# Last self attention in pairs of tiles, and expert results sent by stored numbers

## The reference, cut to what matters

```python
    def _L1_attn_ref(...):            # 16 heads of 128; w = codes * scales, blocks of 32 rows
        q = _mxfp4_matmul(x, wq_codes, wq_scales) + bq
        k = _mxfp4_matmul(x, wk_codes, wk_scales) + bk
        v = _mxfp4_matmul(x, wv_codes, wv_scales) + bv
        scores = jnp.einsum('bqhd,bkhd->bhqk', q, k) / jnp.sqrt(jnp.float32(HEAD_DIM))
        attn = jax.nn.softmax(scores, axis=-1)
        out = jnp.einsum('bhqk,bkhd->bqhd', attn, v).reshape(B, S, NUM_HEADS * HEAD_DIM)
        return _mxfp4_matmul(out, wo_codes, wo_scales) + bo

    def _L1_ffn_ref(...):             # 8 experts, each row goes to its 2 best
        probs = jax.nn.softmax(x @ gate_w, axis=-1)
        gate_score, gate_idx = jax.lax.top_k(probs, TOP_K)
        gate_score = gate_score / jnp.sum(gate_score, axis=-1, keepdims=True)
        combine = jnp.einsum('tk,tke->te', gate_score, onehot) * alpha[None, :]
        h = jax.nn.gelu(jnp.einsum('th,ehi->eti', x, fc1_w) + fc1_b[:, None, :], approximate=False)
        y = jnp.einsum('eti,eih->eth', h, fc2_w) + fc2_b[:, None, :]
        return jnp.einsum('eth,te->th', y, combine)
    ...
    x = x + _L1_attn_ref(_layernorm(x, axis=-1), ...)
    x = x + _L1_ffn_ref(_layernorm(x, axis=-1), ...)
```

## Time and profile before

| | |
|---|---|
| median of 3 runs | 2684.87 us (2684.1 to 2685.65) |
| the profiled execution, its own time | 2690.18 us |
| its span | 2688.5 us |
| mean granted clock of TensorE | 0.98 |
| PE busy | 2534.1 us, 94% |
| PEld busy | 1899.0 us, 71% |
| DVE busy | 1352.2 us, 50% |
| ACT busy | 1269.6 us, 47% |
| POOL busy | 740.1 us, 28% |

### The profile page before, as it was taken

One profiled execution on the slowest core, in us unless ns is written; L12 is line 12 of the kernel. 1 busy time (PEld: TensorE's weight loads), 2 busy tenths in 40 slices (PEclk: granted clock), 3 DMA queues, 4 the chain that ended last, 5 costly groups with the idle time before them and its releaser, 6 DMA issues. The chain is left out here.

```text
span 2688.5 us, 56576 instructions
## 1 busy us (share of the span) xinstructions
PE 2534.1 (94%) x16582; PEld 1899.0 (71%) x16582; DVE 1352.2 (50%) x4786; ACT 1269.6 (47%) x5189; POOL 740.1 (28%) x942
## 2 busy tenths in 40 slices
PE   6999999989899989998899999999879999999797
PEld 5888888878544444445577778777668888888675
DVE  3555555546577744445434455443424444444434
ACT  2555555544466766665546665546412222222142
POOL 1223232347355520003433333321050111111004
PEclk9999999999899999999999999999989999999898
DMA  5322222110510024422445543333280000000033
GB/s 182 78 62 62 65 66 66 53 45 0 166 48 2 1 71 133 128 57 60 131 111 125 138 110 100 96 87 91 99 204 5 8 8 8 8 8 8 18 97 114
DMA packets 171206, 196.01 MB, mean 73 GB/s; under 512 B 34028, under 2 KB 136617, under 8 KB 170307
## 3 DMA queue, kind: packets, MB, share of 16 engines
q1 hardware_dynamic: 142306, 158.49, 20.3%
q0 software_dynamic: 16512, 32.58, 5.4%
q10 hardware_dynamic: 12256, 3.44, 0.8%
HBM read 150.42 MB, written 56.54 MB: 77 GB/s over the span
## 5 line engine op out<-in xcount | busy, mean ns | idle before, releaser
L2276 PE MATMUL sa_work_ps<-sa_xnT,all_big 128*128 128x128 f32 x2048 | 239.7, 279 | 18.1 <-POOL all_big L2609 8.2
L228 PE MATMUL rt_kn_key_ps<-moe_w_wk,all_big 128*128 128x512 f32 x560 | 249.5, 599 | 0.8 <-DVE moe_kn_stats L277 0.4
L2276 PEld LDWEIGHTS sa_work_ps<-sa_xnT,all_big 128*128 128x128 f32 x2048 | 235.2, 195 | 20.5 <-POOL all_big L2609 8.7
L715 ACT ACTIVATE xa_probsT<-xa_probsT_ps 128x256 f32<-128x256 f32 x512 | 191.2, 375 | 95.4 <-PE xa_probsT_ps L580 89.1
L560 PE MATMUL xa_misc_ps<-xa_xnT,cross_folded 128*128 128x256 f32 x1024 | 232.7, 382 | 0.7 <-ACT xa_xnT L681 0.7
L603 PE MATMUL xa_misc_ps<-cross_folded,xa_mixT 128*128 128x256 f32 x1024 | 229.3, 379 | 0.0
L560 PEld LDWEIGHTS xa_misc_ps<-xa_xnT,cross_folded 128*128 128x128 f32 x1024 | 196.0, 191 | 31.5 <-ACT xa_misc_ps L690 3.3
L603 PEld LDWEIGHTS xa_misc_ps<-cross_folded,xa_mixT 128*128 128x128 f32 x1024 | 194.6, 190 | 26.5
L2369 ACT ACTIVATE sa_kT<-sa_work_ps,sa_bias_k 128x128 f32<-128x128 f32 x256 | 73.2, 368 | 294.7 <-PE sa_work_ps L2276 294.7
L580 PE MATMUL xa_probsT_ps<-all_ident,xa_probs 128*128 128x128 f32 x1024 | 197.6, 275 | 4.6 <-DVE xa_probs L841 3.7
L707 ACT ACTIVATE xa_probs<-xa_probs,xa_shift,xa_row_scale 128x257 f32<-128x257 f32 x256 | 152.6, 596 | 90.5 <-DVE xa_shift L825 89.7
(11 more groups left out here) (388 smaller groups left out, 4969.5 us busy)
## 6 DMA issues: line engine op xcount, KB each, us to landing
all_big<-rk SPq DMA_DIRECT2D x256, 128.5 KB
xa_pair<-pairs SPq DMA_DIRECT2D x64, 256.5 KB, 15.1
pairs<-all_big SPq DMA_DIRECT2D x64, 128.5 KB, 3.0
moe_w_wk<-in_ctx_dram SPq DMA_DIRECT2D x64, 128.0 KB, 2.5
pairs<-xa_keys SPq DMA_DIRECT2D x64, 128.0 KB, 2.2
cross_folded<-in_L_ffn_w_gate_dram SPq DMA_DIRECT2D x32, 192.0 KB, 2.5
cross_folded<-in_L_ffn_w_up_dram SPq DMA_DIRECT2D x32, 192.0 KB, 2.7
ff_rows<-pairs SPq DMA_DIRECT2D x35, 128.0 KB, 2.1
```

Source lines behind the costliest of these rows:

```text
L228: pe.matmul(self.key_ps[m % self.banks][0:n, :], self.ctxT[:, c * P:c * P + n], self.wk[:, q * 512:(q + 1) * 512], start=True, stop=True). ...
L715: act.activation(probsT[:, b % 2, :, r * P:(r + 1) * P], probsT_ps[s % 2][:, 0:KB * P].rearrange("p (k n) -> p k n", k=KB), ACT.Copy).then ...
L2276: ins = pe.matmul(ps[:, j, :], w[:, c, h * HD:(h + 1) * HD], xnT[:, c, :], start=(c == 0), stop=(c == NC - 1))
```

## The change

**Attention in pairs.** All working tiles of the attention hold two tiles of rows (`S` = 2, `NP` = 8 pairs). `project_qk` makes q and k for both at once, in eight groups of two heads with products 256 wide; `project_v`, `score`, `mix` and `project_out` run once for each tile of the pair. `iteration` makes q, k, v and scores of pair i + 1 and mix and output of pair i, once plainly and six times in the loop. Routing goes by pairs and one pair behind, so the last sparse pair (6) is routed after the loop, beside the last pair's mix and output. `count` has five small products a pair in place of two a tile. `list_tiles` now follows the last `keep_mix`.

**Sends by stored numbers.** `place` also makes for each choice a number that says where its result belongs (choice, tile, row). GpSimd scatters these numbers, beside the rows, into a second table `expert_ids`, which was filled with a number out of range before; that makes eight indirect DMAs a pair. In `last_experts` SyncE loads with each tile of rows its 128 numbers (two loads a tile, five tiles ahead), and GpSimd sends each `kept` buffer to `expert_out` by them (one indirect DMA a tile), in place of SyncE's store. When all are sent, SyncE loads `expert_out` back with 14 plain loads of 256 KB, two tiles and one choice each; the gathers are gone. `combine` stands behind `add` of experts 2 to 7, two tiles each, the last two after; output is stored two tiles at a time.

**Owners.** TensorE loads the owners' numbers of four tiles with one load, after `turn_rows` and ahead of `second`, in place of one load ahead of each `first`.

**Smaller parts.** The second weights of the feed-forward and the spread second bias are loaded into `spare` and `big`, when their former content is used up. ScalarE runs one Gelu on a gate column at the start of `last_experts`. `stats_of`, `normalize` and `weigh` of the two dense tiles are spread over more steps.

```diff
-ROWS_AHEAD = 6
+LIST = TILES + -TILES % 4
+NO_ONE = 65535
+ROWS_AHEAD = 5
...
-            def project_qk(n, first, route=False):
-                pe.wait_ge(xnT_ready, n + 1)
-                for g in range(NG):
...
+            def project_qk(p, first):
+                pe.wait_ge(xnT_ready, p + 1)
+                for m in range(NS):
+                    if first and m % 2 == 0:
+                        pe.wait_ge(scaled, m + 2)
+                    for w, ps, kept, made in ((wq, work(0, N), q_kept, q_made), (wk, work(1, N), k_kept, k_made)):
...
-            with pe.Fori(1, NT - 1) as i:
+            with pe.Fori(1, NP - 1) as i:
                 iteration(i, True)
-            pe.wait_ge(r_placed, RT)
-            pe.matmul(total_ps, ones[:, :], before[:, :], start=True, stop=True).then_inc(totalled, 1)
-            mix(NT - 1, True)
-            project_out(NT - 1)
+            turn_routed(NP - 2)
+            choose_experts(NP - 2)
+            mix(NP - 1, 0, True)
+            project_out(NP - 1, 0, NP - 2)
+            mix(NP - 1, 1, True)
+            total()
+            project_out(NP - 1, 1)
...
-                dve.wait_ge(scattered, n * (16 * TOP))
+                dve.wait_ge(scattered, p * (32 * TOP * S))
...
+                for t in range(S):
+                    for k in range(TOP):
+                        at = bass.IndirectOffsetOnAxis(ap=places[:, t, k:k + 1], axis=0)
+                        pool.indirect_dma_start(out=expert_rows, out_offset=at, in_=r_xn[:, t, :], in_offset=None,
+                                                bounds_check=E1 * ROOM - 1, oob_is_err=False).then_inc(scattered, 16)
+                        pool.indirect_dma_start(out=expert_ids, out_offset=at, in_=numbers[:, t, k:k + 1], in_offset=None,
+                                                bounds_check=E1 * ROOM - 1, oob_is_err=False).then_inc(scattered, 16)
...
+            def load_owners(j):
+                found = nc.values_load_multi_w_load_instructions(tiles[0:1, 0, j:j + 4], engines=(mybir.EngineType.PE,),
+                                                                 min_val=0, max_val=E1 - 1)[1]
...
             def first(j):
-                owners[j] = pe.value_load(tiles[0:1, 0, j:j + 1], min_val=0, max_val=E1 - 1)
...
+                if j % 4 == 3 and j + 1 < TILES:
+                    load_owners(j + 1)
...
+            act.activation(warmed[:, :], q["gates"][:, 0:1], ACT.Gelu)
...
-            for t in range(RT):
-                for k in range(TOP):
-                    pool.indirect_dma_start(out=got[:, t, k, :], out_offset=None, in_=expert_rows,
-                                            in_offset=bass.IndirectOffsetOnAxis(ap=q["slots"][:, t, k:k + 1], axis=0),
-                                            bounds_check=EXPERT_ROWS - 1, oob_is_err=False).then_inc(gathered[t], 16)
...
+            for j in range(TILES):
+                if j >= ROWS_AHEAD:
+                    pool.wait_ge(rows_loaded[j % ROWS_AHEAD], 32 * (j // ROWS_AHEAD))
+                pool.wait_ge(out_kept, j + 1)
+                apart(pool, passed)
+                pool.indirect_dma_start(out=expert_out, out_offset=bass.IndirectOffsetOnAxis(ap=ids[:, j:j + 1], axis=0),
+                                        in_=kept[:, j % KEPT, :], in_offset=None, bounds_check=TOP * ROOM - 1, oob_is_err=False
+                                        ).then_inc(kept_sent[j % KEPT], 16)
```

641 lines of the change are left out of this document (370 added, 271 removed).

## The result

| | before | after |
|---|---|---|
| median of the runs, us | 2685.26 (2684.1 to 2694.56, 4 runs) | 2716.6 (2715.46 to 2721.92, 4 runs) |
| ratio to before | 1 | 1.0111, 95% interval 1.0094 to 1.0128 |
| the profiled execution, its own time / span | 2690.18 / 2688.5 | 2717.19 / 2715.5 |
| mean granted clock of TensorE | 0.98 | 0.97 |

Left out are one of the two executions of the SyncE version in experiment 6 (3001 us, granted clock 0.84) and one of the kernel before beside it (3795 us, 0.65), both far slower than the same kernels otherwise run.

A forecast was written before the change was run, and what follows sets the result against it. TensorE was taken to bound the kernel, with GpSimd's gathers setting its end. Attention 1.2, sparse part 8.8 and end 11.4 sum to 21.4 us off 2690.2, less 5.3: 2663.5 us median, range 2654 to 2673.

The forecast's parts named there:

- Head: Start of the attention: projecting two tiles together ends the wait for scaled weights; plain iteration starts at 2007.1, gain 10.4 us.
- Loop: Attention loop: a pair takes 69.2 us, eight scatters hide under 69 us; with the head 18.2 us ahead.
- T: End of the last scores of the attention, predicted at 2489.4 us; the drain's steps are timed from it.
- Rival (d): Attention loop stalls: each of 16 groups a pair late by 0.2 us, 22 us, giving 2685.5 us; chance 0.06.
- Loop length: TensorE's attention loop grows from 191 to 321 instructions; by the skill's room for 2048, nothing changes.
- Drain: From the last scores to the next block: 54.3 us, a cost of 17.0 us, bounds 9 and 21.
- Sparse part: Sparse feed-forward, 35 tiles: owners loaded four at a time save 0.25 us a tile, 2.25 us each, gain 8.8.
- Rival (a): Sparse part as before: the load of four stops TensorE like four single ones, or mid waits otherwise; 2672.3 us; chance 0.12.
- (e): Slower: sends through GpSimd pace the sparse part, deciding from 8.2 us a send; 2706 us at 10; chance 0.05.
- End: End of the kernel: plain loads replace 28 gathers; 7.5 us behind TensorE instead of 18.9, gain 11.4.
- rival (c): Loads of results at the end are slow, 114 GB/s: 8.1 us late, 2671.6 us; chance 0.05.
- The sum: Whole kernel: gains of 1.2 + 8.8 + 11.4 = 21.4 us, giving 2668.8 us profiled, 2663.5 us median.

The follow-up runs named there:

- the SyncE version: Kernel before with two plain 128 KB stores more, issued by SyncE beside the scores of each of 14 tiles: 2679.0 us against 2685.4, a single execution.
- experiment 6: Plain stores beside scores: two by SyncE (2679.0 us) or GpSimd (2685.4) in the kernel before; fourteen by GpSimd in the changed kernel with scatters held back (2693.4).
- experiment 2: Kernel before with each tile's 64 score products issued twice: 2751.6 us; with TensorE's loop written out for two tiles: 2729.1 us against 2725.9, ratio 1.0004.
- experiment 1: Changed kernel with the pair's 128 scores split into two bursts of 64, v projection between: 2757.6 us, 1.0117 times before; the unaltered changed kernel took 2759.8.
- experiment 4: Changed kernel with both tiles' scores issued ahead of the count and the last output projection: 2711.4 us, 0.9944 times before, 48.4 less than the unaltered changed kernel.
- experiment 3: Changed kernel with GpSimd's scatters held back until the next pair's scores are through: 2720.7 us, 0.998 times before, 39 less than the unaltered changed kernel.
- experiment 7: Changed kernel with scores ahead of the count and the attention's end reordered: 2703.6 us, 0.9921 times before; on another chip 2670.0 against 2685.4, ratio 0.9951.
- experiment 5: Kernel before with its two scatters a tile held back until they meet the scores: 2765.6 us, 1.015 times before, 41 us slower.
- group 4: Fourth group of runs, on a chip of its own; the unaltered changed kernel took 2711.2 us there, 1.0102 times the kernel before.
- the fourteen stores: Changed kernel with scatters held back past the scores and 14 plain 64 KB stores by GpSimd in their old place: 2693.4 us, 18 less than the unaltered changed kernel.

## Why the prediction was wrong, point by point

- **Head**: right, but in part by luck. The plain iteration starts at 2006.4 (2007.1 predicted), and two misses cancel in it: the first burst of 128 scores already has a stop of 2.16 us in it, and the q and k passes start at 1956.8 and not at 1959.9, since the start didn't slip. The stops in the first two bursts (2.2 and 2.3 us), and a part of that in the third (3.1, the one with scatters across it), are of another kind than those in the loop: at each lies an instruction transfer of 16 KB, and with code that has run before they don't return, as experiment 2 shows from its fourth burst on. No run tests whether the transfer is what they wait for; in experiments 1 and 4 a burst with such a transfer in its last 0.8 us didn't stop. The Trainium skill (Runtime: NRT & Kernel Launch, Instruction fetch mechanics) says that instructions come in blocks of 16 KB and that this is hidden, since they are dispatched more slowly than they are brought in; the transfers' size agrees, but for scores of 20 ns each on code that is new the trace speaks against its being hidden.

The instruction transfers in four stretches of the changed kernel's trace (2002 to 2004, 2071 to 2074, 2144 to 2148, 2160 to 2540; columns: transfers, MB, share of 16 engines):

```profile
q8 instruction: 1, 0.02, 3.5%
...
q8 instruction: 1, 0.02, 2.6%
...
q8 instruction: 1, 0.02, 4.5%
...
q14 instruction: 1, 0.01, 0.0%
```

- **Loop**: the failed step. That "the eight scatters of a pair ... hide under 69 us" priced them at nothing because GpSimd had time for them. It had; but the question was what runs on TensorE while they are issued. The prediction's own numbers put them there: the scores end at T, and it had the last of eight scatters issued at T + 2.5, so they lay across the scores, where before they lay ahead of them. I worked that time out for the landing alone. What it cost: 41 us in six turns, about 5.3 in stopped scores and 1.8 in a sunken clock each; about 2 us of the 41 belong to the first run of the loop's code. Rival (d), loop stalls, had the right kind of loss, but looked for it in the groups of q and k and gave it 0.06; and no rival priced a transfer against TensorE's instructions. The 69.2 us for a pair was right without the coincidence: 68.6 to 69.0 in experiments 3, 4 and 6.
- **Loop length**: right, no effect (experiment 2). Between 2160 and 2540 the trace of the changed kernel has one instruction transfer, where five turns stop. So the rule of the Trainium skill that the prediction cites (Runtime: NRT & Kernel Launch, Instruction fetch mechanics) agrees with the traces: loops of 321 and 382 instructions brought nothing in anew each turn.
- **Drain**: 58.3 where 54.3 was predicted; as a cost 21.0 for 17.0, the upper bound. Up to the last mix each step is right to 1 us (mix of tile 14 at T + 12.6 for 12.4, of tile 15 at T + 30.2 for 30.5), but only since two errors cancel: the price "it lands 2.9 later" was that of a gather, while the ids' scatters took 7.6 (and the rows' 4.5, in the version of experiment 7, from the last issue to the normalisation); and the scatters, which had stopped the scores and with them T, were issued up to T - 1.6 and not T + 2.5. Behind the last mix the ids' landing comes once more, without such a gift: SyncE's first load waits for it, at T + 43.6 for 40.7, and five double loads took 7.5 us for 6.6.
- **Sparse part**: 7.5 us of the 8.8 in the trace, 2.17 us a tile and not 2.25, but two odd waits of 1.0 and 0.4 us, and 2.8 us for the tiles in which the load of four stands, so it wasn't hidden whole. The run without it gives 8.5. Rival (a) is out, and so is (e): the sends never hold a tile up, although GpSimd issues 35 indirect transfers there. Most of its passes there take 0.22 us and the narrow ones come two at a time, so this agrees with experiments 3 and 4.
- **End**: 10.8 of 11.4 us. The loads of results were issued in 8.1 us, and the trace has no wait of VectorE for them; rival (c) is out.
- **The sum**: 42.6 + 4.0 at the attention, 1.3 in the sparse part and 0.5 behind it make the 48.4. Without the coincidence, and with the drain in better order, the kernel comes to 2670.0 on a chip where the kernel before takes 2685.4: 15.4 us gained, where 21.4 had been the forecast.

## What to carry to other kernels

Price a moved DMA by what runs on the other engines while it is issued, not by whether its own engine has time: list for each burst of very short TensorE products which indirect transfers fall on it, before and after. Keep gathers and scatters by GpSimd beside long products (256 columns and more here), and put short ones ahead of the step that releases them; this order of two pieces of one list was worth 48 us, and holding the scatters back instead 39. And when an order is changed on one engine, read each semaphore that its late steps release, for every engine.

## What the runs showed of the hardware

- While GpSimd issued indirect transfers, bursts of passes of 10 ns stopped and passes of 0.22 us did not. On the chip of experiments 1 and 5 TensorE got some five short passes every 0.72 us, by an estimate from these rows one in 0.14 us. On the chips of the result and of group 4 it was less regular: 102 to 188 passes went through, most of them close to full pace, before the first stop of a burst, and single stops lasted 0.2 to 4.3 us. 14 plain stores of 64 KB by GpSimd, two of 128 KB a tile by SyncE, and GpSimd's tensor operations did nothing of the kind.
- From the issue of the last scatter to the step that waits for it took 7.6 us where it was one of 128 ids of 4 bytes, 4.5 where it was one of 128 rows of 1 KB. The ids' packets were through within 2 us of the issue. That the smaller one is slower doesn't hold in general: the medians to landing that the traces of the second run of experiment 7's version and of the fourteen stores give are 5.0 and 4.8 us for ids, 5.3 and 5.2 for rows.
- The granted clock fell to one half 1.3 us into a stop of 3.1 us, and came back some 5 us after TensorE had started again. A stop of 1.57 us (experiment 3, third burst) left the q and k passes behind it at their 27.89 us.
- On code that ran for the first time, bursts of 128 short products stopped for 1.6 to 4.5 us in two or three of the first three, with a 16 KB instruction transfer beside the stops that were looked at; later, with no scatter across them, never.
- Chips differ by 1.5% on the same kernel (2685 and 2725 us), 30 of some 40 us between the two traces of the changed kernel ahead of the attention, and the size of the stops differs too (76.5 and 78.3 us a pair).
